# Attention on one core: the two rows that subtract each query's maximum, for two key tiles and both heads, as four 32-row products in a block of their own

## Chip, cores and metric

The kernel runs on one core of a Trainium2 chip. The metric is the device time of one launch in microseconds (us). Four stages follow each other in that launch: a state-space layer, a quantised linear layer, attention, and a mixture of experts. The change touches attention alone.

## Reference, cut to what matters

```python
x = (latents - mu) * jax.lax.rsqrt(var + 1e-05) * ln_gamma + ln_beta
q = (x @ Wq).reshape(b, s, HEADS, DIM_HEAD).transpose(0, 2, 1, 3)
...
scores = jnp.einsum('bhqd,bhkd->bhqk', q * scale, k * scale)
weights = jax.nn.softmax(scores.astype(jnp.float32), axis=-1).astype(scores.dtype)
out = jnp.einsum('bhqk,bhkd->bhqd', weights, v)
out = out.transpose(0, 2, 1, 3).reshape(b, s, HEADS * DIM_HEAD)
return out @ Wo
```

Here b = 2, s = 2048, 16 heads of 64. The softmax takes each query's maximal score off before the exponential.

## The kernel before, in words

Attention runs once for each of the two batch entries. `attention_first` makes the keys, queries and values of the first pair of heads; `attention_pairs` then does everything else in one long block. Its work is cut into groups `g` (a pair of heads and 512 queries: 8 pairs x 4 pieces = 32 groups) and within a group into 16 units `kt` (128 keys each). One unit is a score tile of 128 keys x 2 heads x 512 queries in two PSUM banks. The banks alternate, so units u and u+1 hold banks 0 to 3.

The order on TensorE (PE) is written out by hand, two units a turn, in the loop at the end of its block:

- `maxes(u)`: 2 products of 64 rows (one for each head, in two halves of the array's rows) that are read by VectorE (DVE) for the maxima of the next group (`find_max`, L976; `read_max`, L983). They wait until DVE has read the step before (`max_read`); there is only one pair of banks for it.
- `scores(u + 2)`, `scores(u + 3)`: four terms each (L1202): main keys x main queries, main x rest, rest x main, and `row_ones` x `row_shift`. The last term adds minus the maximum: `row_shift` holds it in two rows (a rough part and a correction) in rows 0, 1 for head 0 and 64, 65 for head 1; all other rows are zero. Each term is a pair of products of 64 rows. The unit's last product raises `s_psum`.
- `maxes(u + 1)`.
- `values(u)`, `values(u + 1)`: products of the exponentials `p` with v (L1213), 128 rows by 64 columns, one for each head; the trace shows two passes of each, so 8 to a turn.
- at six of a group's eight turns (`BANK7_AT`, by kt) one use of bank 7: the denominators (kt 2, L1224), the output product (kt 8, L1229), the turned shift of the next group (kt 10, `turn_shift`, L1000), or a projection of later heads (kt 0, 12, 14, L1009 or L1011). It waits for `bank7_free`.

ScalarE (ACT) makes `p` of a unit from its two banks (L1299) and copies bank 7 out where needed (the shift at L1273). GpSimd (POOL) adds the `p` of a group's 16 units up (L1323, 15 adds a group, eight `p` buffers deep). DVE reads each maximum step, and at kt 10 runs `make_shift` (L990 to L992) ahead of that unit's `read_max`; it also does `rest_part` (L1019) behind the read of an odd unit, which frees bank 7, and the steps of the division (L1344, L1345, L1351).

The semaphore of a score unit is counted by ACT:

```python
for i, (left, right) in enumerate(terms):
    for h in range(2):
        last = nc.tensor.matmul(s_bank(u)[:, piece(h)], left[hi(h)], right[hi(h)],
                                start=(i == 0), stop=(i == len(terms) - 1))
last.then_inc(s_psum, 1)
```

Of the kernel before, what the change touches and what calls it, by code (L numbers as in the profile page):

```python
# [17 lines left out]
BF16 = mybir.dt.bfloat16  # L18
U32 = mybir.dt.uint32
ALU = mybir.AluOpType  # L20
ACT = mybir.ActivationFunctionType
X_AXIS = mybir.AxisListType.X

P = 128
BANK = 512
# [3 lines left out]
TPC = BANK // P  # L29
# [795 lines left out]
def phase2(nc, ins, x_in, x_out, experts, ident, ident_bf, ones, exponent, psum):  # L825


    with Phase(nc) as ph:
        xaT = ph.sbuf("xaT", [P, SEQ])
        attnT = ph.sbuf("attnT", [P, SEQ])  # L830
        stat = ph.sbuf("stat2", [P, 4, TILES])
        six = ph.sbuf("six2", [P, TILES, 6])
        two = ph.sbuf("two2", [P, TILES, 2])
        gamma = ph.sbuf("gamma", [P, 1])
        beta = ph.sbuf("beta", [P, 1])
        w_qkv = ph.sbuf("w_qkv", [P, 2, 3, P])
        w_o = ph.sbuf("w_o", [P, 2, D])

        v = ph.sbuf("v", [P, 2, TILES, P])

        k_main = ph.sbuf("k_main", [P, 2, SEQ], F32R)
        k_rest = ph.sbuf("k_rest", [P, 2, SEQ], F32R)
        q_main = ph.sbuf("q_main", [P, 2, SEQ], F32R)
        q_rest = ph.sbuf("q_rest", [P, 2, SEQ], F32R)

        row_shift = ph.sbuf("row_shift", [P, 2, BANK], F32R)
        row_ones = ph.sbuf("row_ones", [P, P], F32R)  # L850
        quarters = ph.sbuf("quarters", [P, 2, 2, PAIR_MAXES])

        o_raw = ph.sbuf("o_raw", [P, BANK])
        den_g = ph.sbuf("den_g", [P, 2, 2, BANK])
        rec = ph.sbuf("rec", [P, BANK])
        newt = ph.sbuf("newt", [P, BANK])
        common = {k: x for k, x in locals().items() if k not in ("nc", "x_in", "x_out", "ins", "ph", "experts")}

        with Phase(nc) as su:
            zero_one = su.sbuf("zero_one", [P, 2])  # L860
            loaded, filled, cleared, step = (su.sem(s) for s in ("loaded", "filled", "cleared", "step"))
            with nc.Block() as block:
                @block.sync
                def _(sp):
                    sp.dma_start(gamma[:], ins["ln_gamma"]).then_inc(loaded, 16)
                    sp.dma_start(beta[:], ins["ln_beta"]).then_inc(loaded, 16)
                    sp.wait_ge(loaded, 32)

                @block.gpsimd
                def _(pool):  # L870
                    nc.gpsimd.memset(experts["down_b"][:], 0.0).then_inc(cleared, 1)
                    pool.wait_ge(cleared, 1)

                @block.vector
                def _(dve):
                    st = Steps(dve, step)

                    st.link(nc.vector.memset(zero_one[:, 0:1], 0.0))
                    st.link(nc.vector.memset(zero_one[:, 1:2], 1.0))
                    for i in range(2):  # L880
                        nc.vector.tensor_copy(row_shift[:, i, :], zero_one[:, 0:1].to_broadcast([P, BANK])).then_inc(filled, 1)
                    nc.vector.tensor_copy(row_ones[:], zero_one[:, 0:1].to_broadcast([P, P])).then_inc(filled, 1)
                    dve.wait_ge(filled, 3)
                    for h in range(2):
                        nc.vector.tensor_copy(row_ones[64 * h:64 * h + 2, :],
                                              zero_one[64 * h:64 * h + 2, 1:2].to_broadcast([2, P])).then_inc(filled, 1)
                    dve.wait_ge(filled, 5)
            nc.all_engine_barrier(sems_to_clear=sem_range(su.sems))

        for b in range(BATCH):  # L890
            attention_input(nc, ins, x_in, b, common)
            attention_first(nc, b, common, experts if b == 0 else None)
            attention_pairs(nc, ins, b, common)
            attention_output(nc, x_in, x_out, b, common)
# [54 lines left out]
PAIR_MAXES = TPC * CHUNKS  # L949

AHEAD = 6
SHIFT_MADE_AT = PAIR_MAXES - AHEAD

BANK7_AT = {0: 0, 2: "den", 8: "out", 10: "shift", 12: 1, 14: 2}
# [8 lines left out]
def hi(h):  # L963

    return slice(64 * h, 64 * h + 64)


def piece(c):
    return slice(c * BANK, (c + 1) * BANK)
# [16 lines left out]
def make_shift(nc, st, quarters, maxima, shift):  # L986


    each = quarters.rearrange("p h (j k) -> p (h j) k", k=CHUNKS)
    st.mark(nc.vector.tensor_reduce(maxima, each, X_AXIS, ALU.max, negate=True))  # L990
    st.link(nc.vector.tensor_reduce(shift[:, :, 0], each, X_AXIS, ALU.max, negate=True))
    return nc.vector.tensor_tensor(shift[:, :, 1], maxima, shift[:, :, 0], ALU.subtract)  # L992


def turn_shift(nc, dst, shift, ident_bf):

    for h in range(2):
        at = 64 * h
        for j in range(TPC):
            last = nc.tensor.matmul(dst[at:at + 2, j * P:(j + 1) * P], shift[:, h * TPC + j, :], ident_bf[:],  # L1000
                                    start=True, stop=True)
    return last

# [17 lines left out]

def attention_first(nc, b, m, experts):

    xaT, w_qkv, w_o, v, k_main, k_rest, q_main, q_rest, row_shift, quarters, ident_bf, psum = (
        m[k] for k in "xaT w_qkv w_o v k_main k_rest q_main q_rest row_shift quarters ident_bf psum".split())
    with Phase(nc, f"_{b}") as su:
        maxima = su.sbuf("maxima0", [P, 2 * TPC])
        shift = su.sbuf("shift0", [P, 2 * TPC, 2], BF16)
        (step, proj_psum, rounded, raw_ready, rest_done_v, rest_done_g, v_read, max_psum, max_read, shift_ready,
         shift_psum, shift_read) = (su.sem(s) for s in (  # L1030
            "step proj_psum rounded raw_ready rest_done_v rest_done_g v_read max_psum max_read shift_ready "
# [7 lines left out]
        km, kr, qm, qr = (t[:, 0] for t in (k_main, k_rest, q_main, q_rest))  # L1039
        with nc.Block() as block:  # L1040
# [39 lines left out]
            def _(act):  # L1080
# [10 lines left out]
                act.wait_ge(shift_psum, 1)  # L1091
                for h in range(2):
                    at = 64 * h
                    nc.scalar.copy(row_shift[at:at + 2, 0, :], psum[at:at + 2, 0:BANK]).then_inc(shift_read, 1)
                act.wait_ge(rounded, 2 * CHUNKS)
                act.wait_ge(v_read, CHUNKS)
                act.wait_ge(shift_read, 2)
# [18 lines left out]
def attention_pairs(nc, ins, b, m):  # L1116


    xaT, attnT, w_qkv, w_o, v, k_main, k_rest, q_main, q_rest, ones, ident_bf, psum = (
        m[k] for k in "xaT attnT w_qkv w_o v k_main k_rest q_main q_rest ones ident_bf psum".split())  # L1120
    row_shift, row_ones, quarters = (m[k] for k in "row_shift row_ones quarters".split())
    o_raw, den_g, rec = (m[k] for k in "o_raw den_g rec".split())
    GC = PAIRS * CHUNKS
    units = [(g, kt) for g in range(GC) for kt in range(KT)]
# [18 lines left out]
    with Phase(nc, f"_{b}") as su:  # L1143
        p = su.sbuf("p", [P, LIVE, 2, BANK])
        maxima = su.sbuf("maxima", [P, 2 * TPC])
        shift = su.sbuf("shift", [P, 2 * TPC, 2], BF16)
        (weights, out_weight, step, max_psum, max_read, shift_ready, shift_read, s_psum, p_ready, pv_done, added_g,
         o_copied, rec_rough, rec_step, rec_ready, o_ready, rounded, bank7_full, bank7_free) = (
            su.sem(s) for s in (
# [12 lines left out]
        with nc.Block() as block:  # L1162
# [16 lines left out]
            def _(pe):  # L1179
# [10 lines left out]
                def scores(u):  # L1190
                    g, kt = units[u]
                    km, kr, qm, qr = buffers(g, k_main, k_rest, q_main, q_rest)
                    if kt == 0 and g:
                        pe.wait_ge(shift_read, 2 * g)
                    if u >= 2:
                        pe.wait_ge(p_ready, u - 1)
                    keys, cols = slice(kt * P, (kt + 1) * P), piece(g % CHUNKS)
                    terms = [(km[:, keys], qm[:, cols]), (km[:, keys], qr[:, cols]), (kr[:, keys], qm[:, cols]),
                             (row_ones[:], row_shift[:, g % 2, :])]
                    for i, (left, right) in enumerate(terms):  # L1200
                        for h in range(2):
                            last = nc.tensor.matmul(s_bank(u)[:, piece(h)], left[hi(h)], right[hi(h)],  # L1202
                                                    start=(i == 0), stop=(i == len(terms) - 1))
                    last.then_inc(s_psum, 1)

                def values(u):
                    g, kt = units[u]
# [31 lines left out]

                scores(0)  # L1240
                scores(1)
                for u in range(0, len(units), 2):
                    maxes(u)
                    if u + 2 < len(units):
                        scores(u + 2)
                        scores(u + 3)
                    maxes(u + 1)
                    values(u)
                    values(u + 1)
                    if u in at_unit:  # L1250
                        use_bank7(at_unit[u])

            @block.scalar
            def _(act):
                nc.scalar.preload_act_table_set(EXP_LN)

                def read_bank7(k):
# [12 lines left out]
                    elif what == "shift":  # L1270
                        for h in range(2):
                            at = 64 * h
                            nc.scalar.copy(row_shift[at:at + 2, (g + 1) % 2, :], bank7[at:at + 2, :]).then_inc(shift_read, 1)  # L1273
                        act.wait_ge(shift_read, 2 * (g + 1))
                        nc.scalar.nop().then_inc(bank7_free, 1)
                    else:
# [541 lines left out]
```

## Time and profile before

| | us |
|---|---|
| median of 3 runs | 3752.65 (3745.63 to 3760.2) |
| the profiled execution, its own time | 3751.12 |
| its span, first to last instruction | 3749.0 |
| mean granted TensorE clock, share of full | 0.951 |

The span is one execution by the hardware profiler. PE is the matmul row, PEld the weight loads, which overlap it. A matmul's end is modelled, so its start is what to read: the distance of two starts is what a product takes. "Idle before" is time the engine stood, with what released it.

### The profile page before, as it was taken

To read this page: it belongs to the slowest core of one execution; us is meant where nothing else is said; L and a number is where in the kernel's file an instruction comes from. 1 tells how busy PE (TensorE), PEld (TensorE's weight loads), DVE (VectorE), ACT (ScalarE), POOL (GpSimd) and SP (SyncE) were. 2 spreads that over 40 slices of the span, in tenths; PEclk is the share of its full clock that TensorE was granted. 3 is DMA by queue.
4 is the path that set the end of the run, shared out by engine and by line. 5 is a ranking of instruction groups with operands and counts; after the bars stand their busy time and mean duration, and the time that the engine had idled before them with its cause. 6 is when DMAs were issued, how large, how long until landed. Compare 5 with 4: busy or idle time off the path is not lost. (4 is left out here: it accounts for less than half of the span.)

```text
span 3749.0 us, 48401 instructions
## 1 busy us (share of the span) xinstructions
PE 3371.6 (90%) x19041; PEld 1777.9 (47%) x19041; DVE 2386.7 (64%) x2724; ACT 1686.7 (45%) x2081; POOL 2762.5 (74%) x1154
## 2 busy tenths in 40 slices
PE   5774688289999999999999499999999999998898
PEld 2222233245554545555455245455554545554798
DVE  5998699766666666665664556656666666662554
ACT  4331433145454454454445244454445454454454
POOL 1883188158888888888889288888888888898233
PEclk9897798689999999999999799999999999998899
DMA  1330233010000000000000100000000000000000
GB/s 25 135 118 28 59 120 104 28 28 1 4 1 4 4 1 4 1 4 1 2 1 1 40 3 1 4 4 1 4 1 4 1 4 2 1 1 12 26 18 15
DMA packets 61535, 76.14 MB, mean 20 GB/s; under 512 B 7289, under 2 KB 48962, under 8 KB 61250
## 3 DMA queue, kind: packets, MB, share of 16 engines
q1 hardware_dynamic: 59362, 72.71, 6.1%
q8 instruction: 146, 2.39, 0.3%
q14 instruction: 75, 0.61, 0.1%
q10 hardware_dynamic: 1952, 0.43, 0.1%
HBM read 66.30 MB, written 6.82 MB: 20 GB/s over the span
## 5 line engine op out<-in xcount | busy, mean ns | idle before, releaser
L1323 POOL TENSOR_TENSOR den_g<-den_g,p 128x1024 f32<-128x1024 f32 x896 | 2128.6, 2376 | 288.5 <-ACT p L1299 183.0
L983 DVE TENSOR_REDUCE quarters<-psum 128x2 f32<-128x1024 f32 x1024 | 1250.6, 1224 | 939.3 <-PE psum L976 929.3
L1299 ACT ACTIVATE p<-psum 128x1024 f32<-128x1024 f32 x1024 | 994.5, 1023 | 725.4 <-PE psum L1202 717.3
L1213 PE MATMUL psum<-p,v 128*64 128x512 f32 x4096 | 991.6, 605 | 0.0
L976 PE MATMUL psum<-k_main,q_main 64*128 64x512 f32 x2048 | 462.4, 446 | 13.7 <-DVE quarters L983 11.2
L1213 PEld LDWEIGHTS psum<-p,v 128*64 128x64 f32 x4096 | 248.4, 136 | 470.0 <-issue 316.1
L1202 PE MATMUL psum<-q_main,k_main 64*128 64x512 f32 x2048 | 408.1, 394 | 4.5 <-PEq L1113 4.5
L1202 PE MATMUL psum<-q_rest,k_main 64*128 64x512 f32 x2048 | 405.1, 391 | 0.0
L1202 PE MATMUL psum<-q_main,k_rest 64*128 64x512 f32 x2048 | 404.8, 390 | 0.0
L1202 PE MATMUL psum<-row_shift,row_ones 64*128 64x512 f32 x2048 | 404.5, 390 | 0.0
L976 PEld LDWEIGHTS psum<-k_main,q_main 64*128 64x128 f32 x2048 | 193.7, 184 | 361.3 <-issue 198.6
L726 POOL TENSOR_TENSOR seen<-state,c_sb 128x2048 f32<-128x2048 f32 x64 | 285.2, 4457 | 68.6 <-DVE state L673 60.2
L611 PE MATMUL psum<-seen,ident 128*128 128x512 f32 x512 | 264.7, 654 | 26.9 <-POOL seen L726 26.8
L1202 PEld LDWEIGHTS psum<-q_main,k_main 64*128 64x128 f32 x2048 | 194.9, 186 | 42.3 <-issue 11.3
L1202 PEld LDWEIGHTS psum<-q_main,k_rest 64*128 64x128 f32 x2048 | 194.4, 185 | 43.1
L1202 PEld LDWEIGHTS psum<-q_rest,k_main 64*128 64x128 f32 x2048 | 194.4, 185 | 42.6
L1202 PEld LDWEIGHTS psum<-row_shift,row_ones 64*128 64x128 f32 x2048 | 194.2, 185 | 42.8
L1323 POOL TENSOR_TENSOR den_g<-p 128x1024 f32<-128x1024 f32 x64 | 151.0, 2360 | 55.4 <-ACT p L1299 54.2
L713 POOL TENSOR_TENSOR xnT<-dx,work 128x1024 f32<-128x1024 f32 x32 | 75.2, 2349 | 153.7 <-DMA work<-bc_rows 153.7
L611 PEld LDWEIGHTS psum<-seen,ident 128*128 128x128 f32 x512 | 96.2, 201 | 153.0 <-issue 103.5
L1009 PE MATMUL psum<-xaT,w_qkv 128*128 128x512 f32 x256 | 147.9, 667 | 6.9 <-PEq L942 4.0
L1775 POOL TENSOR_TENSOR mixed<-mixed,part 128x512 f32<-128x512 f32 x56 | 74.1, 1323 | 104.3 <-DVE part L1740 104.3
(253 smaller groups left out, 3298.2 us busy)
## 6 DMA issues: line engine op xcount, KB each, us to landing
c_sb<-bc_rows SPq DMA_DIRECT2D x64, 512.0 KB, 3.6
work<-bc_rows SPq DMA_DIRECT2D x32, 512.0 KB, 4.8
resid<-in_resid SPq DMA_DIRECT2D x8, 256.0 KB, 3.8
x_mid<-resid SPq DMA_DIRECT2D x8, 256.0 KB, 2.6
xa<-x_mid SPq DMA_DIRECT2D x8, 256.0 KB, 3.6
x_tok<-x_mid SPq DMA_DIRECT2D x8, 256.0 KB, 3.8
x_mid<-x_tok SPq DMA_DIRECT2D x8, 256.0 KB, 2.7
x<-x_mid SPq DMA_DIRECT2D x8, 256.0 KB, 2.8
```

The costliest lines, as they stand in the source:

```text
L611: last = nc.tensor.matmul(y_sum[:, h, k * BANK:(k + 1) * BANK], ident[:], seen[:, i % SLOTS, h, k * BANK:(k + 1) * BANK], start=False, sto ...
L713: nc.gpsimd.tensor_tensor(fed[:, k % SLOTS, :], dx[:, 1, s * SCAN:(s + 1) * SCAN], b_sb[:, k % SLOTS, :], ALU.mult).then_inc(fed_by_pool, 1)
L726: nc.gpsimd.tensor_tensor(seen[:, i % SLOTS, 0:halves], state[:, i % SLOTS, 0:halves], c_sb[:, i % C_SLOTS, :].unsqueeze(1).to_broadcast([ ...
L976: last = nc.tensor.matmul(max_banks[:, piece(h)], q[hi(h), c * BANK + j * P:c * BANK + (j + 1) * P], k[hi(h), piece(quarter)], start=True, ...
L983: return nc.vector.reduce_max(quarters[:, :, n], max_banks.rearrange("p (h k) -> p h k", h=2), X_AXIS)
L1009: return nc.tensor.matmul(dst, w[:, 1 - i // CHUNKS, :], xaT[:, piece(c)], start=True, stop=True)
L1202: last = nc.tensor.matmul(s_bank(u)[:, piece(h)], left[hi(h)], right[hi(h)], start=(i == 0), stop=(i == len(terms) - 1))
L1213: last = nc.tensor.matmul(o_bank[hi(h), :], vv[:, kt, hi(h)], p[:, u % LIVE, h, :], start=(kt == 0), stop=(kt == KT - 1))
L1299: nc.scalar.activation(flat(p[:, u % LIVE]), s_bank(u), ACT.Exp, scale=float(DH) ** -0.5).then_inc(p_ready, 1)
L1323: nc.gpsimd.tensor_tensor(sums, first, src, ALU.add).then_inc(added_g, 1)
L1775: nc.gpsimd.tensor_tensor(mixed[:, u % 2], x[:, u % 2] if e == 0 else mixed[:, u % 2], part[:, e % 2], ALU.add).then_inc(summed, 1)
```

## The change

Three things, all in attention:

- The fourth term leaves `scores`. `subtract_maxima(u)` does it for units u and u+1 and both heads as four products of 32 rows each, in the four quarters of the array's rows: quarter 2h + v takes head h of unit u + v. It stands once a turn, behind `maxes(u + 1)` and ahead of `values(u)`. One product of it raises `s_psum` by 2, so ACT hears of both units at once. The wait for the next group's shift moves there too.
- The two rows of each head are needed in two quarters now. `make_shift` writes columns 0, 1 and 32, 33 of a `shift` tile that is 34 wide and zero between: one reduction and one subtraction more. `turn_shift` turns 34 columns instead of 2, and ACT copies 34 rows instead of 2.
- `shift` is one tile of the whole stage, zeroed once by POOL, and `row_ones` gets its ones in four places instead of two, once.

```diff
-        shift = su.sbuf("shift", [P, 2 * TPC, 2], BF16)
+        shift = ph.sbuf("shift", [P, 2 * TPC, SHIFT_ROWS], BF16)
...
+                nc.gpsimd.memset(shift[:], 0.0).then_inc(cleared, 1)
...
-                    for h in range(2):
-                        nc.vector.tensor_copy(row_ones[64 * h:64 * h + 2, :],
+                    for r in range(4):
+                        nc.vector.tensor_copy(row_ones[32 * r:32 * r + 2, :],
...
+SHIFT_ROWS = 34
...
     st.mark(nc.vector.tensor_reduce(maxima, each, X_AXIS, ALU.max, negate=True))
-    st.link(nc.vector.tensor_reduce(shift[:, :, 0], each, X_AXIS, ALU.max, negate=True))
-    return nc.vector.tensor_tensor(shift[:, :, 1], maxima, shift[:, :, 0], ALU.subtract)
+    for at in (0, 32):
+        st.mark(nc.vector.tensor_reduce(shift[:, :, at], each, X_AXIS, ALU.max, negate=True))
+    st.wait()
+    st.mark(nc.vector.tensor_tensor(shift[:, :, 1], maxima, shift[:, :, 0], ALU.subtract))
+    return nc.vector.tensor_tensor(shift[:, :, 33], maxima, shift[:, :, 32], ALU.subtract)
...
-            last = nc.tensor.matmul(dst[at:at + 2, j * P:(j + 1) * P], shift[:, h * TPC + j, :], ident_bf[:],
+            last = nc.tensor.matmul(dst[at:at + SHIFT_ROWS, j * P:(j + 1) * P], shift[:, h * TPC + j, :], ident_bf[:],
...
-                    if kt == 0 and g:
-                        pe.wait_ge(shift_read, 2 * g)
...
-                             (row_ones[:], row_shift[:, g % 2, :])]
...
-                    last.then_inc(s_psum, 1)
+                def subtract_maxima(u):
+                    g, kt = units[u]
+                    if kt == 0 and g:
+                        pe.wait_ge(shift_read, 2 * g)
+                    for v in range(2):
+                        for h in range(2):
+                            rows = slice(64 * h + 32 * v, 64 * h + 32 * v + 32)
+                            last = nc.tensor.matmul(s_bank(u + v)[:, piece(h)], row_ones[rows, :], row_shift[rows, g % 2, :],
+                                                    start=False, stop=True)
+                    last.then_inc(s_psum, 2)
...
                 scores(1)
+                subtract_maxima(0)
                 for u in range(0, len(units), 2):
...
                     maxes(u + 1)
+                    if u + 2 < len(units):
+                        subtract_maxima(u + 2)
                     values(u)
...
-                            nc.scalar.copy(row_shift[at:at + 2, (g + 1) % 2, :], bank7[at:at + 2, :]).then_inc(shift_read, 1)
+                            nc.scalar.copy(row_shift[at:at + SHIFT_ROWS, (g + 1) % 2, :], bank7[at:at + SHIFT_ROWS, :]).then_inc(shift_read, 1)
```

## Rows read from the trace of the kernel before

**Rows 1.** Each engine's busy time, share of the span, instructions.

```profile
PE 3371.6 (90%) x19041; PEld 1777.9 (47%) x19041; DVE 2386.7 (64%) x2724; ACT 1686.7 (45%) x2081; POOL 2762.5 (74%) x1154
```

**Rows 2.** Busy time in a stretch of attention: PE, PEld, DVE, ACT, POOL, clock, DMA.

```profile
1000.00:1500.00 500.00, 498.72 (x3069) 253.35 (x3070) 312.69 (x308) 248.81 (x295) 436.99 (x185) 1.00 0.01 3
```

**Rows 3.** The costliest groups: count, busy us, mean ns, idle before.

```profile
L1323 POOL TENSOR_TENSOR den_g<-den_g,p 128x1024 f32<-128x1024 f32 x896 | 2128.6, 2376 | 288.5 <-ACT p L1299 183.0
L1202 PE MATMUL psum<-row_shift,row_ones 64*128 64x512 f32 x2048 | 404.5, 390 | 0.0
```

**Rows 4.** Timeline, one turn without bank 7 (kt 4): start us, us, engine.

```profile
1005.69 0.50 PE L976 MATMUL psum<-k_main,q_main 64*128 64x512 f32 x2
...
1006.03 0.40 PE L1202 MATMUL psum<-q_main,k_main 64*128 64x512 f32 x2
...
1006.24 1.23 DVE L983 TENSOR_REDUCE quarters<-psum 128x2 f32<-128x1024 f32 x1 [1.61 <-PE psum L976]
...
1007.16 1.94 ACT L1299 ACTIVATE p<-psum 128x1024 f32<-128x1024 f32 x2
...
1007.64 0.39 PE L1202 MATMUL psum<-row_shift,row_ones 64*128 64x512 f32 x2
1007.64 0.19 PEld L976 LDWEIGHTS psum<-k_main,q_main 64*128 64x128 f32 x2
1007.87 0.39 PE L976 MATMUL psum<-k_main,q_main 64*128 64x512 f32 x2
1008.18 0.20 PEld L1213 LDWEIGHTS psum<-p,v 128*64 128x64 f32 x4 [0.35 <-ACT p L1299]
...
1009.09 0.14 PEld L1213 LDWEIGHTS psum<-p,v 128*64 128x64 f32 x2 [0.29 <-issue]
...
1010.05 0.50 PE L976 MATMUL psum<-k_main,q_main 64*128 64x512 f32 x2
```

**Rows 5.** Timeline, the last two value products of that turn.

```profile
1009.52 0.60 PE L1213 MATMUL psum<-p,v 128*64 128x512 f32 x2
```

**Rows 6.** Timeline, the turn before it (kt 2), which ends with bank 7.

```profile
1002.70 0.20 PEld L1213 LDWEIGHTS psum<-p,v 128*64 128x64 f32 x4 [0.35 <-ACT p L1299]
...
1003.95 0.68 DVE L1019 TENSOR_TENSOR k_rest<-psum,k_main 128x512 fp32r<-128x512 f32 x1
1004.68 0.20 PEld L1224 LDWEIGHTS psum<-den_g,ones 128*64 128x64 f32 x4 [0.93 <-DVE k_rest L1019]
```

**Rows 7.** Waits, whole span: us in total, times, longest.

```profile
PEld psum L1009 <- DVE q_rest L1019: 26.1, 28, 0.9
...
PEld psum L1224 <- DVE k_rest L1019: 24.3, 26, 0.9
```

**Rows 8.** The instructions of line 992: shortest, median, longest ns.

```profile
L992 DVE TENSOR_TENSOR shift<-maxima,shift x64: 170/2100/2144, 780.9 to 3401.4; 128x8 bf16<-128x8 f32 x64
```

**Rows 9.** Timeline, `make_shift` and the turn of kt 10.

```profile
1018.35 4.90 POOL L1323 TENSOR_TENSOR den_g<-den_g,p 128x1024 f32<-128x1024 f32 x2
1018.36 0.19 DVE L990 TENSOR_REDUCE maxima<-quarters 128x8 f32<-128x32 f32 x1
1018.46 0.18 DVE L991 TENSOR_REDUCE shift<-quarters 128x8 bf16<-128x32 f32 x1
1018.67 2.07 DVE L992 TENSOR_TENSOR shift<-maxima,shift 128x8 bf16<-128x8 f32 x1
...
1019.90 0.50 PE L976 MATMUL psum<-k_main,q_main 64*128 64x512 f32 x2
...
1020.66 1.21 DVE L983 TENSOR_REDUCE quarters<-psum 128x2 f32<-128x1024 f32 x1
```

**Rows 10.** Timeline, later in that turn.

```profile
1021.92 0.19 PEld L976 LDWEIGHTS psum<-k_main,q_main 64*128 64x128 f32 x2
1022.08 0.39 PE L976 MATMUL psum<-k_main,q_main 64*128 64x512 f32 x2
```

**Rows 11.** Timeline, POOL's next add.

```profile
1020.86 2.40 POOL L1323 TENSOR_TENSOR den_g<-den_g,p 128x1024 f32<-128x1024 f32 x1
```

More of the change, by code:

```diff
@@ L871, in _ @@
                     nc.gpsimd.memset(experts["down_b"][:], 0.0).then_inc(cleared, 1)
-                    pool.wait_ge(cleared, 1)
+                    nc.gpsimd.memset(shift[:], 0.0).then_inc(cleared, 1)
+                    pool.wait_ge(cleared, 2)
                 @block.vector
@@ L883, in _ @@
                     dve.wait_ge(filled, 3)
-                    for h in range(2):
-                        nc.vector.tensor_copy(row_ones[64 * h:64 * h + 2, :],
-                                              zero_one[64 * h:64 * h + 2, 1:2].to_broadcast([2, P])).then_inc(filled, 1)
-                    dve.wait_ge(filled, 5)
+                    for r in range(4):
+                        nc.vector.tensor_copy(row_ones[32 * r:32 * r + 2, :],
+                                              zero_one[32 * r:32 * r + 2, 1:2].to_broadcast([2, P])).then_inc(filled, 1)
+                    dve.wait_ge(filled, 7)
             nc.all_engine_barrier(sems_to_clear=sem_range(su.sems))
@@ L1022, in attention_first @@
 def attention_first(nc, b, m, experts):
-    xaT, w_qkv, w_o, v, k_main, k_rest, q_main, q_rest, row_shift, quarters, ident_bf, psum = (
-        m[k] for k in "xaT w_qkv w_o v k_main k_rest q_main q_rest row_shift quarters ident_bf psum".split())
+    xaT, w_qkv, w_o, v, k_main, k_rest, q_main, q_rest, row_shift, quarters, shift, ident_bf, psum = (
+        m[k] for k in "xaT w_qkv w_o v k_main k_rest q_main q_rest row_shift quarters shift ident_bf psum".split())
     with Phase(nc, f"_{b}") as su:
         maxima = su.sbuf("maxima0", [P, 2 * TPC])
-        shift = su.sbuf("shift0", [P, 2 * TPC, 2], BF16)
         (step, proj_psum, rounded, raw_ready, rest_done_v, rest_done_g, v_read, max_psum, max_read, shift_ready,
@@ L1093, in _ @@
                     at = 64 * h
-                    nc.scalar.copy(row_shift[at:at + 2, 0, :], psum[at:at + 2, 0:BANK]).then_inc(shift_read, 1)
+                    nc.scalar.copy(row_shift[at:at + SHIFT_ROWS, 0, :], psum[at:at + SHIFT_ROWS, 0:BANK]).then_inc(shift_read, 1)
                 act.wait_ge(rounded, 2 * CHUNKS)
@@ L1120, in attention_pairs @@
         m[k] for k in "xaT attnT w_qkv w_o v k_main k_rest q_main q_rest ones ident_bf psum".split())
-    row_shift, row_ones, quarters = (m[k] for k in "row_shift row_ones quarters".split())
+    row_shift, row_ones, quarters, shift = (m[k] for k in "row_shift row_ones quarters shift".split())
     o_raw, den_g, rec = (m[k] for k in "o_raw den_g rec".split())
@@ L1197, in scores @@
                     keys, cols = slice(kt * P, (kt + 1) * P), piece(g % CHUNKS)
-                    terms = [(km[:, keys], qm[:, cols]), (km[:, keys], qr[:, cols]), (kr[:, keys], qm[:, cols]),
-                             (row_ones[:], row_shift[:, g % 2, :])]
+                    terms = [(km[:, keys], qm[:, cols]), (km[:, keys], qr[:, cols]), (kr[:, keys], qm[:, cols])]
                     for i, (left, right) in enumerate(terms):
                         for h in range(2):
-                            last = nc.tensor.matmul(s_bank(u)[:, piece(h)], left[hi(h)], right[hi(h)],
-                                                    start=(i == 0), stop=(i == len(terms) - 1))
-                    last.then_inc(s_psum, 1)
+                            nc.tensor.matmul(s_bank(u)[:, piece(h)], left[hi(h)], right[hi(h)], start=(i == 0), stop=False)
+                def subtract_maxima(u):
[8 more added lines that the diff above has]
+                    last.then_inc(s_psum, 2)
                 def values(u):
```

## The prediction

> **What bounds the kernel.** I read the page's busy shares first: PE 90%, POOL 74%, DVE 64%, ACT 45% [rows 1]. These are averages over four stages, so I then read the busy time of stretches inside attention. There PE is busy for 498.7 of 500 us at the full granted clock (2.4 GHz) and POOL for 437 [rows 2]. Attention's line 992 runs from 780.9 to 3401.4 [rows 8], so some 2600 us of the span go at PE's pace. A microsecond taken from PE's list in a turn is a microsecond of the end, until something else ends last. The next candidate is POOL: an add takes 2.38 us, and the next starts 2.51 behind it [rows 3, 9, 11], so 185 instructions fill 464 of the 500 us. Attention can lose 7% before POOL is the bound. The list of costly groups gives the term that is moved: 2048 products of `row_shift`, none with idle time before it [rows 3].
>
> Then the timeline of one plain turn, for starts alone [rows 4, 5]. From its first `maxes` to the next turn's are 4.36 us. Pairs of 64-row products stand 0.23 us apart (1006.03 to 1007.64 is seven of them). Value pairs stand 0.43 apart (1009.09 to 1009.52). And the places where the array's division changes cost more than a pair: values to `maxes` 1009.52 to 1010.05 is 0.53 for a pair of 0.43, and the first `maxes` pair to the first score pair 0.34 for a pair of 0.23. In the other direction, `maxes` to values is 1007.87 to 1008.18, 0.31 for 0.23.
>
> **The change part by part.**
>
> *Shift products.* A turn has two pairs of them, 0.46 us. In their place stands one block of four products in four quarters. Two halves run side by side now (both starts within one row of the timeline); if four quarters do so too, the block takes 0.23. Gain 0.23 a turn, 512 turns: **-118 us**.
>
> *The block's own entry.* Before, the turn had two changes of division: 128 rows to 64, and 64 rows to 128 x 64. Now it has three: 128 to 64, 64 to 32 rows, 32 rows to 128 x 64. The trace has no change from 64 to 32 rows. Nearest is the one into a row division, 128 to 64: 0.10 before the first product and 0.11 on it, because the weights of 128 columns are loaded in the open; 0.21 together [rows 4, 5]. The block loads 128 columns as well. I take 0.21: **+108 us**. Lower bound 0, if quarters count as the same division as halves. Middle bound the other direction's 0.08 and 0.05 (0.13), with 64 columns to load: +67. Upper bound 0.32, if the four weight loads go two by two and the open load doubles: +164.
>
> The Trainium skill ("TensorEngine Tiling (Array Packing)", § Key Properties) says that a change of tiling mode drains TensorE, while another tile of one mode does not. By that rule the three changes each drain, which is the 0.21 taken and not the lower bound of 0; the page has no price for a drain, and this trace's changes agree that each costs something.
>
> *Stalls on bank 7.* After an odd `read_max`, DVE runs `rest_part` (0.68 us), and only then is bank 7 free. At 1004.63 it ends, and PE's load for L1224 starts at 1004.68 [rows 6]. Without it the values, begun at 1002.70, would let it start 1.77 later (as 1008.18 to 1009.52 plus 0.43), at 1004.47. So PE stands 0.21. There are 26 such waits in one row for L1224 and 14 in a second row behind `q_rest`; for L1009 28, and another 28 behind `k_rest` [rows 7]. Those of L1009 need a new division anyway, which takes 0.10 of the 0.21, so they cost about 0.11: 40 x 0.21 + 56 x 0.11 = 14.6, and a few of L1011, 16 in all. In the changed turn the block stands between `maxes(u + 1)` and the values and makes PE 0.44 later there (0.23 + 0.21), while DVE's chain hangs on `maxes(u + 1)` alone. The stalls go: **-16 us**. If the entry costs nothing, PE is 0.23 later and they go just as well.
>
> *The read between the two `maxes`.* `maxes(u + 1)` may load its weights when DVE has read the step before. DVE starts 0.55 behind `maxes(u)`, reads 1.23 and ends at 1007.47; the load stands at 1007.64, of which 0.05 is the semaphore's way (as 1004.63 to 1004.68) [rows 4, 6]. So 0.12 is spare. With the pair gone the load wants to start 0.23 earlier and is 0.11 late. But it is issued 0.23 ahead of its product, and needs some 0.11 of these (the open load above), so it can be 0.12 late for nothing. At kt 10 this is seen: the load at 1021.92, only 0.16 ahead of its product at 1022.08, with no pair pushed out [rows 10]. I cost it at nothing; the cover is nearly used up.
>
> *Exponentials.* The first unit's signal now comes with the second's. Before, ACT starts at 1007.16, 1.47 into the turn. Now the block starts 1.72 + 0.31 = 2.03 into it, and ACT 0.54 behind (as DVE behind the first `maxes`), at 2.6. Two exponentials of 1.94 in all end at 4.5 [rows 4]. The next turn's second score unit needs the second one's end, and its load would stand 0.8 into that turn, at 5.1. Spare 0.6. POOL gets its `p` 1.1 later, with eight buffers and 7% to spare. ACT's bank 7 work comes after the turn's end, behind 4.5. Cost nothing.
>
> *The shift's own path.* `make_shift` has one reduction more (0.10, L990 to L991) and one subtraction more. A subtraction takes 170 ns at best and 2100 in the median [rows 8]. The reason stands in the timeline: L992 starts at 1018.67 and ends at 1020.74, as POOL's add begun at 1018.35 ends (2.38 later, 1020.73). It waits for the add, then, though no semaphore joins the two [rows 9]. So what the second one costs depends on who is next. DVE's next instruction starts at 1020.66, POOL's next add at 1020.86 [rows 9, 11]. A second subtraction of 0.17 from 1020.66 on would end at 1020.83, just before. I take it as fitting the gap: 0.1 us on DVE, ahead of a read that in this kernel starts 0.2 late without harm. If it doesn't fit, it waits for a whole add (a rival, below).
>
> *The rest.* `turn_shift` turns 34 columns instead of 2, eight times a group: between -0.10 a group (a division nearer to that of the values) and +0.2 (longer loads in the open), -6 to +12 us over all; I take 0. ACT's copies have 512 elements a row as before. The wait for the next group's shift stands in the same turn of kt 14 as before, but 1.7 us later in it, so the copy has more time than before; the values would be queued behind it. Three small instructions of preparation, once: under 1 us.
>
> **Sum:** -118 + 108 - 16 = -26 us, from the profiled execution's 3751.1 to 3725. The median of the runs lies 1.5 above that execution: 3726.5.
>
> **The rivals.**
>
> *R1, the second subtraction waits for a whole add of POOL* (the other side). It would then end 2.51 behind the first. The first ends 0.84 into the turn of kt 10 now (1020.74 less 1019.90 [rows 9]). The adds move 1.1 later against the turn with the exponentials, and an add's end then falls at 0.84 + 1.1 - 2.51, 0.57 ahead of the turn; the first takes that one, the second the next, 1.94 into the turn. The read starts at 1.86 instead of 0.55 and ends at 3.1, the load follows at 3.15, the product 0.11 later at 3.26 instead of 1.72: 1.5 late, once a group. About 55 of 64 groups have POOL busy there (median 2100 ns [rows 8]): +83, **3809 us**. For it: the gap is only 0.14 to 0.2 us. Against: DVE asks first. The Trainium skill ("SBUF — State Buffer", § Who interferes with whom) states a lock on a shared port pair that the first to start holds for its whole instruction; the 2.1 against 0.17 us agrees, and asking first would spare the second subtraction. It decides if the second subtraction takes over 1 us.
>
> *R2, entering quarters is free.* Then only the gain stands: -118 - 16, **3618 us**. Against: every change of division that the trace has costs something.
>
> *R3, four quarters don't run side by side at full pace.* If two by two, the block takes 0.46: +118, 3844 us; half of that, **3785 us**. For it: the trace shows no more than two row parts, and four would write four PSUM banks at a time. Against: two parts lose nothing.
>
> The Trainium skill ("TensorE: Matmul & The Clock Gate", § Measured speedup vs the span model) gives 3.07 times for four row tiles, not 4. An estimate from that: the block would take 0.30 and not 0.23, the sum some +10, 3763 us.
>
> *R4, the maximum's read becomes a wait.* If a late load isn't hidden, each turn loses 0.11 at `maxes(u + 1)`: +55, **3781 us**. It decides when DVE's read ends later than some 1.8 into the turn.
>
> **Numbers.** Forecast (entry at about 0.21, the rest hidden) 50%, with its own range 3700 to 3748: the entry's price is uncertain by 0.04 a turn or 20 us. R1 15%, R2 10%, R3 14%, R4 8%, others 3%. The 8 in 10 range leaves out R2 and the far end of R3: 3690 to 3815. A measurement of this kernel can tell some 0.5% from no change, 19 us, so under 3734 is faster. Of the forecast's 50 some 32 lie there, with R2 and others 44%. Slower (over 3771): R1, most of R3, two thirds of R4 and little else, 30%. The same: 26%.
>
> **What would show it.** Right: a plain turn of about 4.34 us; the block's first start 0.31 behind `maxes`, the values some 0.43 behind that; no start on L1224 waiting for `rest_part`; the second subtraction at 0.1 to 0.2 us. Wrong: values 0.65 or more behind the block (R3), a second subtraction of 2 us with DVE's read of kt 10 late (R1), the load of `maxes(u + 1)` right behind DVE's end with its product pushed out (R4), a block start 0.23 behind `maxes` (R2), or a POOL that never idles in a group.

## The result and the profile after

The changed kernel takes 3820.88 us (median of 4 runs, 3817.73 to 3825.63) against 3752.06 for the kernel before on the same chip: 1.0179 times as long, 95% interval 1.0166 to 1.0193. It is 69 us slower, where 26 us faster was forecast.

First the busy time of the stretch of attention that [rows 2] show of before (PE, PEld, DVE, ACT, POOL, clock), and the group of the moved products:

```profile
1000.00:1500.00 500.00, 500.00 (x2996) 230.65 (x2992) 293.15 (x324) 240.81 (x287) 425.65 (x181) 1.00 0.01 3
```

```profile
L1217 PE MATMUL psum<-row_shift,row_ones 32*128 32x512 f32 x2048 | 259.7, 497 | 0.0
```

PE is "busy" for all 500 us, more than the 498.7 of before, and yet does fewer products in them (2996 for 3069; POOL 181 instructions for 185). The granted clock is the same, 1.00 of full. A matmul's end is modelled, and one that waits for its weights is drawn longer (497 ns here, 390 in [rows 3]), so such a stall can't be seen in the busy share or in "idle before". It is seen in the starts. Timeline of the changed kernel, one turn, here with a bank 7 use at its end:

```profile
1007.20 0.50 PE L981 MATMUL psum<-k_main,q_main 64*128 64x512 f32 x2
...
1007.54 0.39 PE L1206 MATMUL psum<-q_main,k_main 64*128 64x512 f32 x2
...
1007.74 1.23 DVE L988 TENSOR_REDUCE quarters<-psum 128x2 f32<-128x1024 f32 x1 [1.97 <-PE psum L981]
...
1008.69 0.40 PE L1206 MATMUL psum<-q_main,k_rest 64*128 64x512 f32 x2
1009.02 0.19 PEld L981 LDWEIGHTS psum<-k_main,q_main 64*128 64x128 f32 x2 [0.37 <-DVE quarters L988]
1009.02 0.51 PE L981 MATMUL psum<-k_main,q_main 64*128 64x512 f32 x2
1009.46 0.19 PEld L1217 LDWEIGHTS psum<-row_shift,row_ones 32*128 32x128 f32 x4 [0.25 <-issue]
1009.46 0.51 PE L1217 MATMUL psum<-row_shift,row_ones 32*128 32x512 f32 x4
...
1009.90 0.20 PEld L1228 LDWEIGHTS psum<-p,v 128*64 128x64 f32 x4 [0.25 <-issue]
...
1010.01 1.94 ACT L1317 ACTIVATE p<-psum 128x1024 f32<-128x1024 f32 x2 [2.12 <-PE psum L1217]
```

Read against [rows 4]. The first `maxes` to the first score pair: 0.34, as before. The last score pair to the second `maxes`: 1008.69 to 1009.02, 0.33 where pairs stand 0.23 apart. The weights of `maxes` are loaded at 1009.02, not a pair earlier, and this is 0.05 behind the end of DVE's read (1007.74 + 1.23 = 1008.97). Second `maxes` to the block: 0.44, where 0.31 was expected. Block to values: 0.44, as expected.

The waits of the whole span, as [rows 7] show them of before, and the two subtractions of the shift (ns, shortest, median, longest), for [rows 8]:

```profile
PEld psum L981 <- DVE quarters L988: 227.0, 548, 0.8
...
PEld psum L1239 <- DVE k_rest L1028: 12.9, 26, 0.5
```

```profile
L999 DVE TENSOR_TENSOR shift<-maxima,shift x64: 194/756/1260, 786.9 to 3475.1; 128x8 bf16<-128x8 f32 x64
```

```profile
L1000 DVE TENSOR_TENSOR shift<-maxima,shift x64: 178/180/186, 787.0 to 3476.2; 128x8 bf16<-128x8 f32 x64
```

DVE's read now releases the load of `maxes` 548 times, once a turn and some, for 227.0 us of idle load; before it was 172 times and 120.0 us. The loads of the denominators (L1224 before) stand idle 12.9 us in 26 waits instead of 24.3, 0.44 less each, which is what the block ahead of the values takes on PE. The second subtraction never waits.

### The profile page after: what moved, and what is told of

It is laid out like the page before. It is cut to its first block and busy times, and to the rows that moved or that the text cites. A ratio compares the mean times of both kernels' runs of the same rounds, so it can differ in the third digit from the quotient of the medians.

```text
span 3821.3 us, 48470 instructions
## 1 busy us (share of the span) xinstructions
PE 3450.7 (90%) x19041; PEld 1689.3 (44%) x19041; DVE 2340.1 (61%) x2854; ACT 1680.6 (44%) x2081; POOL 2763.2 (72%) x1155
## 5 line engine op out<-in xcount | busy, mean ns | idle before, releaser
L981 PE MATMUL psum<-k_main,q_main 64*128 64x512 f32 x2048 | 512.9, 497 | 14.3 <-DVE quarters L988 11.6
L1217 PE MATMUL psum<-row_shift,row_ones 32*128 32x512 f32 x2048 | 259.7, 497 | 0.0
L1217 PEld LDWEIGHTS psum<-row_shift,row_ones 32*128 32x128 f32 x2048 | 98.0, 181 | 128.3 <-issue 128.3
```

The lines of the kernel that those rows point to most:

```text
L981: last = nc.tensor.matmul(max_banks[:, piece(h)], q[hi(h), c * BANK + j * P:c * BANK + (j + 1) * P], k[hi(h), piece(quarter)], start=True, ...
L1217: last = nc.tensor.matmul(s_bank(u + v)[:, piece(h)], row_ones[rows, :], row_shift[rows, g % 2, :], start=False, stop=True)
```

## The experiments

Theory A, formed on these rows: the change took *two* pairs of products out of the stretch between a turn's two maximum steps (the fourth term of both score units), so the second step now waits for DVE. Rival B: the block of quarters, or its late signal to ACT, is what costs. Each experiment below is held against the kernel before, run beside it on the same chip.

**Shorter read, in the changed kernel.** DVE reads 256 of 512 scores a head; the maxima of the other keys are left out.

```diff
-    return nc.vector.reduce_max(quarters[:, :, n], max_banks.rearrange("p (h k) -> p h k", h=2), X_AXIS)
+    return nc.vector.reduce_max(quarters[:, :, n], max_banks.rearrange("p (h k) -> p h k", h=2)[:, :, 0:256], X_AXIS)
```

> The changed kernel, but DVE's maximum read takes 256 of each head's 512 scores (the maxima of the other half of the keys are left out), so it is some 0.55 us shorter and can't hold the second maximum step. Theory A (two score pairs, not one, left the stretch between the two maximum steps, so the second one now waits for DVE's read, 0.10 us a turn, and its weights are loaded in the open, 0.11 more): some 490 turns give back 0.21 us each, 3821 to about 3718. Rival B (the cost lies in the block of four quarters itself or in its late signal to ACT): the read plays no part, 3800 to 3825.

**The control: the same edit in the kernel before.**

> The control: the kernel before with the same shortened read. No turn waits for the read there, so both theories expect only what the earlier freeing of bank 7 gives: 3752 to about 3736. If it drops by much more, the read held the kernel before too and the first experiment can't be put down to the new wait.

Measured: 3710.4 us in the changed kernel, 0.9892 of before (0.9875 to 0.9908), 110 us under the changed one. The control: 3720.4, 0.9921 (0.9905 to 0.9938). The timeline of a plain turn (one without bank 7) of the first:

```profile
1006.69 0.50 PE L981 MATMUL psum<-k_main,q_main 64*128 64x512 f32 x2
1007.23 0.69 DVE L988 TENSOR_REDUCE quarters<-psum 128x2 f32<-128x512 f32 x1 [0.71 <-PE psum L981]
...
1008.19 0.19 PEld L981 LDWEIGHTS psum<-k_main,q_main 64*128 64x128 f32 x2
1008.41 0.39 PE L981 MATMUL psum<-k_main,q_main 64*128 64x512 f32 x2
1008.73 0.19 PEld L1217 LDWEIGHTS psum<-row_shift,row_ones 32*128 32x128 f32 x4 [0.35 <-issue]
...
1009.17 0.20 PEld L1228 LDWEIGHTS psum<-p,v 128*64 128x64 f32 x4 [0.25 <-issue]
...
1011.03 0.51 PE L981 MATMUL psum<-k_main,q_main 64*128 64x512 f32 x2
```

The load stands 0.22 ahead of its product again, `maxes` to block is 0.32, and the turn 4.34 us: what the prediction had said of the changed kernel. The block and its late signal are still there, so B is out as the cause of the loss. The control fell by 29 where 16 was expected. Most of the rest lies ahead of the turns: from the first maximum step to the first value product that kernel takes 26.8 us, the kernel before 34.0, in each of the two batch entries. The changed kernel gains there too: 35.2 and 35.1 us fall to 30.2 and 27.9, 12 in all. So not all of its 110 us is the wait. The wait's own share is read in the turns: the 486 that each trace has from one first `maxes` to the next take 2518.6 us in the changed kernel and 2418.0 with the short read, 0.21 less each (2453.1 before, 2431.7 in the control). Lines 976 and 1213 of the control; the two times behind the durations are the first and the last start:

```profile
L976 PE MATMUL psum<-k_main,q_main x2048: 383/492/790, 766.2 to 3367.9; 64*128 64x512 f32 x187
```

```profile
L1213 PEld LDWEIGHTS psum<-p,v x4096: 132/137/137, 793.0 to 3413.3; 128*64 128x64 f32 x196
```

With the short read in both, the changed kernel is 10.0 us ahead. About 5 of these lie in the turns of kt 10, where the wider shift is turned (60 of them, 4.60 us on average against 4.69). A plain turn takes 4.35 us on average against 4.38. So the block itself wins a few hundredths of a us a turn at most, as the prediction's two large terms have it (118 - 108 = 10 us).

**The move alone.** The kernel before, its fourth term behind the second `maxes`, as two pairs of 64 rows.

```diff
-                    terms = [..., (row_ones[:], row_shift[:, g % 2, :])]
...
+                def subtract_maxima(u):
...
+                    for v in range(2):
+                        for h in range(2):
+                            last = nc.tensor.matmul(s_bank(u + v)[:, piece(h)], row_ones[hi(h)], row_shift[hi(h), g % 2, :],
+                                                    start=False, stop=True)
+                    last.then_inc(s_psum, 2)
```

> The kernel before with the shift's products moved behind the second maximum step but left as two pairs of 64 rows (no quarters, no new division of the array, one signal for both units, 2 columns of shift). Theory A: the stretch between the maximum steps is as short as in the changed kernel, the wait of 0.10 and the open load of 0.11 are both paid, the stalls on bank 7 go: 3752 + 105 - 16 = about 3840. Rival B (quarters are what costs): near 3740.

Measured: 3843.2, 1.0247 (1.023 to 1.0264), as expected. The move alone costs 94 us, with no quarter in it. From its timeline:

```profile
1008.82 0.40 PE L1199 MATMUL psum<-q_main,k_rest 64*128 64x512 f32 x2
1009.14 0.19 PEld L976 LDWEIGHTS psum<-k_main,q_main 64*128 64x128 f32 x2 [0.36 <-DVE quarters L983]
1009.14 0.49 PE L976 MATMUL psum<-k_main,q_main 64*128 64x512 f32 x2
...
1009.48 0.63 PE L1207 MATMUL psum<-row_shift,row_ones 64*128 64x512 f32 x4
```

0.32 to the second `maxes` and 0.34 from it to the next pair, for 0.23 each: 0.09 of waiting and 0.11 of load in the open.

**Quarters ahead of the second maximum step.**

```diff
-                    maxes(u + 1)
                     if u + 2 < len(units):
                         subtract_maxima(u + 2)
+                    maxes(u + 1)
```

> The changed kernel with the block of quarters ahead of the second maximum step instead of behind it. The distance between the two maximum steps is long enough again, so no wait for the read, but the array is divided anew four times a turn instead of three (32 rows back to 64). Theory A with a division at 0.20 us: a plain turn of 4.55 us against 4.56 in the changed kernel and some stalls on bank 7 back, 3820 to 3835. If going from 32 to 64 rows were free, about 3735.

Measured: 3845.7, 1.0252 (1.0235 to 1.0269), slower than expected. Its timeline:

```profile
905.46 0.39 PE L1206 MATMUL psum<-q_main,k_rest 64*128 64x512 f32 x2
905.78 0.19 PEld L1217 LDWEIGHTS psum<-row_shift,row_ones 32*128 32x128 f32 x4 [0.36 <-issue]
...
906.22 0.50 PE L981 MATMUL psum<-k_main,q_main 64*128 64x512 f32 x2
...
906.65 0.20 PEld L1228 LDWEIGHTS psum<-p,v 128*64 128x64 f32 x4 [0.25 <-issue]
...
908.43 0.19 DVE L999 TENSOR_TENSOR shift<-maxima,shift 128x8 bf16<-128x8 f32 x1
...
908.52 2.37 DVE L1000 TENSOR_TENSOR shift<-maxima,shift 128x8 bf16<-128x8 f32 x1
909.57 0.19 PEld L981 LDWEIGHTS psum<-k_main,q_main 64*128 64x128 f32 x2 [0.76 <-issue]
...
910.79 1.21 DVE L988 TENSOR_REDUCE quarters<-psum 128x2 f32<-128x1024 f32 x1
...
912.06 0.49 PE L981 MATMUL psum<-k_main,q_main 64*128 64x512 f32 x2 [0.17 <-DVE quarters L988]
```

The wait for the read is gone in a plain turn, but each of the block's two borders costs: 0.32 into it, and 0.44 and 0.43 behind it for products of 0.23. Of 0.44, 0.11 is the open load and 0.10 the change of division. So quarters ask for some 0.20 a time at either place. The plain turn comes out at 4.55 us, as expected; what was not expected lies in the other turns. The rival R1 of the prediction turns up, in the second part of the rows: POOL's add starts at 908.43, as the first subtraction does. The first is through in 0.19, the second meets the add and takes 2.37, and the read of kt 10 and the second `maxes` (2.49 behind the first) are late. So it goes in 36 of the 64 groups. The stalls on bank 7 are back too, 0.93 us of idle load each as before. POOL's row in the same timeline, and the waits of the span:

```profile
908.43 2.40 POOL L1341 TENSOR_TENSOR den_g<-den_g,p 128x1024 f32<-128x1024 f32 x1
```

```profile
PEld psum L1239 <- DVE k_rest L1028: 24.2, 26, 0.9
```

**That kernel with one subtraction over two columns**, to try R1.

```diff
-    st.mark(nc.vector.tensor_tensor(shift[:, :, 1], maxima, shift[:, :, 0], ALU.subtract))
-    return nc.vector.tensor_tensor(shift[:, :, 33], maxima, shift[:, :, 32], ALU.subtract)
+    return nc.vector.tensor_tensor(shift[:, :, 1:34:32], maxima.unsqueeze(2).to_broadcast([P, 2 * TPC, 2]),
+                                   shift[:, :, 0:33:32], ALU.subtract)
```

> The kernel with the block of quarters ahead of the second maximum step, and both subtractions of the shift as one instruction over two columns. In the run with two, the first was mostly free (0.19 us) and the second waited for POOL's add (median 2.37), which held the read of kt 10 and made that turn 5.03 us instead of 4.78. If it is the second instruction's wait (the rival R1 of the prediction), one instruction is free here and the turn of kt 10 falls to about 4.78: 0.25 x 60, 3846 to about 3831. If the adds just stand in another phase and the one instruction waits as well, 3846.

Measured: 3844.5, 1.0244 (1.0229 to 1.026). Inconclusive as to the time, where 3831 was expected: in 37 of the 64 groups the one instruction was free, in the other 27 it met the add itself. The turn of kt 10 does show R1's price: 4.78 us in the median, with the instruction free, against 5.03 with two subtractions, and 4.86 against 4.99 on average, 8 us in 60 turns. Which way it goes is a matter of hundredths of a us: where the add had started 0.01 to 0.03 us ahead of the subtraction this took 2.4 us, where it started just behind it 0.20.

```profile
L999 DVE TENSOR_TENSOR shift<-maxima,shift x64: 202/205/2422, 783.3 to 3494.8; 128x16 bf16<-128x16 f32 x64
```

**A wait between the two subtractions, in the changed kernel.**

```diff
-    st.mark(nc.vector.tensor_tensor(shift[:, :, 1], maxima, shift[:, :, 0], ALU.subtract))
+    st.link(nc.vector.tensor_tensor(shift[:, :, 1], maxima, shift[:, :, 0], ALU.subtract))
```

> The changed kernel with a semaphore wait between the two subtractions of the shift. In the changed kernel the second takes 0.18 us each time. If what saved it is that it asks for its input ahead of POOL's next add, the wait's some 0.1 us lets the add in: the second subtraction then takes up to 2.4 us in groups where the first waited for an add, and DVE's read behind it is late. If the two never compete, 0.18 again.

Measured in a single run: 3819.0 us. The second subtraction:

```profile
L1000 DVE TENSOR_TENSOR shift<-maxima,shift x64: 194/196/197, 784.5 to 3471.4; 128x8 bf16<-128x8 f32 x64
```

Still free, so the wait did not let the add in. The semaphore moved the second subtraction 0.14 us back, and it still starts 0.05 us ahead of POOL's next add and ends while this is under way. A subtraction behind one that has waited for an add gets through in POOL's gap, with room for a semaphore. What waits is the instruction that comes while an add is under way.

**The block doubled, with zero weights first.**

```diff
+                    for ones_or_none in (row_none, row_ones):
...
-                            last = nc.tensor.matmul(s_bank(u + v)[:, piece(h)], row_ones[rows, :], row_shift[rows, g % 2, :],
-                                                    start=False, stop=True)
+                                last = nc.tensor.matmul(s_bank(u + v)[:, piece(h)], ones_or_none[rows, :],
+                                                        row_shift[rows, g % 2, :], start=False, stop=(ones_or_none is row_ones))
```

> The changed kernel with the block of four quarters doubled: four more products with zero weights ahead of the four, in the same division. It prices the block without its entry. If four quarters run side by side at full pace: 0.23 us a turn, 512 turns, 3821 + 117 = about 3938. If two by two: +236, about 4057.

Measured: 3934.8, 1.0481 (1.0465 to 1.0497): 114 us over the changed kernel, 0.22 a turn, which is what one pair of halves takes. Four quarters run side by side at full pace, and R3 is out. Its timeline has the first block's open load (0.34 to the second) and the change to the values (0.33):

```profile
1001.76 0.50 PE L1220 MATMUL psum<-row_shift,row_none 32*128 32x512 f32 x4
...
1002.10 0.40 PE L1220 MATMUL psum<-row_shift,row_ones 32*128 32x512 f32 x4
1002.43 0.20 PEld L1231 LDWEIGHTS psum<-p,v 128*64 128x64 f32 x4 [0.37 <-issue]
```

**The kernel before with the second maximum step one pair earlier.**

```diff
                     for i, (left, right) in enumerate(terms):
+                        if i == len(terms) - 1 and ahead_of_shift is not None:
+                            maxes(ahead_of_shift)
                         for h in range(2):
...
-                        scores(u + 3)
-                    maxes(u + 1)
+                        scores(u + 3, u + 1)
+                    else:
+                        maxes(u + 1)
```

> The kernel before with the second maximum step one pair earlier, ahead of the last shift pair of the second score unit. It tests the cover: its load then waits for DVE's read 0.11 us, of which the 0.12 by which a load may be late should hide all; and DVE's chain behind it frees bank 7 0.23 us earlier, so its stalls go. Cover as reckoned: 3752 - 16 = about 3736. Cover too short: up to 0.1 us a turn lost, up to 3790.

**The same with 34 columns of shift**, 32 of them zero (ACT copies two rows as before, one subtraction).

> The kernel before with the second maximum step one pair earlier (as in the run before) and the shift turned with 34 columns instead of 2, 32 of them zero, so that its products stand in the division of the values ahead of them (the changed kernel shows 0.42 instead of 0.52 us there). 0.10 us a group more off: about 3730, if the early step gives its 16.

Measured: 3749.2, 0.9991 (0.9982 to 1.0), and 3742.3, 0.9968 (0.9956 to 0.998). The early step gave 3 us, not 16. The lead of the load covers the wait, as reckoned: in a plain turn the load starts 0.13 ahead of its product instead of 0.22, no product is late, and the turn stays at 4.38 us on average. The stall on bank 7 is gone as well, which gives some 15 us. But the turn of kt 10 is not free: 4.89 us on average instead of 4.70, 12 us in 60 turns. Timeline of the second of these kernels there:

```profile
980.47 2.35 DVE L996 TENSOR_TENSOR shift<-maxima,shift 128x8 bf16<-128x8 f32 x1
981.93 0.19 PEld L980 LDWEIGHTS psum<-k_main,q_main 64*128 64x128 f32 x2 [0.76 <-issue]
...
982.71 1.21 DVE L987 TENSOR_REDUCE quarters<-psum 128x2 f32<-128x1024 f32 x1
...
983.98 0.19 PEld L980 LDWEIGHTS psum<-k_main,q_main 64*128 64x128 f32 x2 [0.37 <-DVE quarters L987]
```

The subtraction starts just after an add of POOL has started, and takes as long as that does; the read begins 0.78 into the turn instead of the 0.55 of a plain turn, and the load waits for it, now that the spare time is spent.

**And with the subtraction on POOL**, in its queue behind the add of kt 10.

```diff
                     nc.gpsimd.tensor_tensor(sums, first, src, ALU.add).then_inc(added_g, 1)
                     n += 1
+                    if kt == SHIFT_MADE_AT and g + 1 < GC:
+                        pool.wait_ge(reduced, 2 * (g + 1))
+                        nc.gpsimd.tensor_tensor(shift[:, :, 1], maxima[:], shift[:, :, 0], ALU.subtract).then_inc(shift_ready, 1)
```

> The kernel with the early maximum step and the wide turned shift, and the shift's subtraction on POOL, in its queue behind the add of kt 10, instead of on DVE. In the run without this the subtraction waited 2.34 us on DVE and the turn of kt 10 took 4.82 us instead of some 4.60. If that wait is what ate the 16 us of the freed bank 7, 0.22 x 60 = 13 us come back: 3742 to about 3729, 0.6% below the kernel before. If not, 3742.

Measured: 3737.6, 0.9954 (0.994 to 0.9967), the fastest of the kernels that compute everything. Its timeline at kt 10:

```profile
983.33 0.50 PE L980 MATMUL psum<-k_main,q_main 64*128 64x512 f32 x2
983.87 1.23 DVE L987 TENSOR_REDUCE quarters<-psum 128x2 f32<-128x1024 f32 x1 [2.04 <-PE psum L980]
984.10 0.24 POOL L1332 TENSOR_TENSOR shift<-maxima,shift 128x8 bf16<-128x8 f32 x1
...
985.14 0.19 PEld L980 LDWEIGHTS psum<-k_main,q_main 64*128 64x128 f32 x2
985.28 0.39 PE L980 MATMUL psum<-k_main,q_main 64*128 64x512 f32 x2
985.71 1.23 DVE L987 TENSOR_REDUCE quarters<-psum 128x2 f32<-128x1024 f32 x1
```

The read starts 0.54 into the turn, the load is back 0.14 ahead of its product. The turns of kt 10 fall from 4.79 to 4.61 us on average, 11 us in 60 of them, near the 13 expected. Of these the whole kernel shows about 5 (0.9954 against 0.9968, each held against its own runs of the kernel before, and with intervals that overlap); where the rest went stays open.

## Why the prediction was wrong

The step that failed is "The read between the two `maxes`". It says: "With the pair gone the load wants to start 0.23 earlier and is 0.11 late", and costs that at nothing. Between the two `maxes` of a turn lie both score units, and each lost its shift pair. The load wants to start 0.46 earlier, 1.49 into the turn, and DVE's read lets it go at 1.82. It is 0.33 late, of which 0.12 is hidden by the lead of a load over its product; 0.21 is left, twice what R4 asked for. The paragraph on exponentials had the right figure, the second `maxes` at 1.72 into the turn, which is 0.46 and not 0.23 earlier than before; the two weren't set against each other.

Term by term:

- Shift products, -118: held. The doubled block cost 114.
- Entry into quarters, +108: held, though 0.21 was carried over from another change of division. With the wait gone, `maxes` to block is 0.32 and block to values 0.44 in the plain turn, and the turn 4.34 us.
- Stalls on bank 7, -16: held. In the move alone, and in the changed kernel, they are gone; in the kernel with quarters ahead of the step they are back. The 16 may be somewhat low: the turns of the control gained 21 us.
- Read between the steps, 0: was 0.21 us a turn, in some 490 turns (those with a second maximum step), +103. The short read took 101 us out of the 486 turns of the trace.
- Exponentials, 0: held. ACT starts 2.81 into the turn and ends its two at 4.75, later than the 4.5 reckoned by the same 0.21.
- Second subtraction, nothing: held here (0.18 us each time). R1's mechanism is real and hangs on where POOL's add stands: in the kernel with quarters ahead it cost the turn of kt 10 0.25 us where it struck.
- `turn_shift`, 0 within -6 to +12: its first product stands 0.42 behind the last value pair instead of 0.52, so at 62 groups it gave 6 us, the near bound.

With the mended terms: -118 + 108 - 16 - 6 + 103 = +71. Measured +69. That the two meet within 2 us is partly luck, since the terms are good to a few us each.

R4 was the right rival, at half its price and with a chance of only 8%. One of its signs was right: the load of `maxes(u + 1)` right behind DVE's end, with its product pushed out. The other was not ("when DVE's read ends later than some 1.8 into the turn"): that end did not move, it stands 1.78 into the turn before and 1.77 after, and yet each turn waits. The need for it moved. With two pairs gone, the load is late for nothing up to 1.49 + 0.12 = 1.61 into the turn, so the read would have to end by 1.56.

The Trainium skill ("TensorEngine Tiling (Array Packing)", § Key Properties) says that a change of tiling mode drains TensorE. The runs agree that such a change costs, from 64 to 32 rows and from 32 to 64: about 0.10 us each, besides 0.11 for a load that isn't made ahead across it. The estimate from the 3.07 times of the Trainium skill ("TensorE: Matmul & The Clock Gate", § Measured speedup vs the span model) would have made the block 0.30 us; the doubled block shows 0.22.

## What to carry to other kernels

When work is taken out of a hand-written order, count what leaves each stretch between two uses of a single buffer, not what leaves the loop: a reader on another engine doesn't get faster, and the time saved in that stretch comes back as a wait for it, with the next weight load in the open on top. Packing products into more, smaller row tiles saves one product's time and pays a change of division at the border (here 0.23 against 0.20), so it should be worth doing only where several such products stand together. The doubled block shows the second one at 0.22 with no border of its own; no run here shows a kernel that gains by it and computes everything.

## What the runs showed of the hardware

- A weight load may come late by some of its lead of 0.23 us over its product: 0.09 late cost nothing (the kernel with the early step, 4.38 us a turn as before), and 0.12 is what the sums give. When it was 0.33 late, the product started 0.10 later, and its own load in the open added 0.11: 0.21 us a turn.
- A DVE instruction of 0.2 us with two SBUF inputs takes up to 2.4 when it comes during a POOL add, while one that follows it takes 0.18 to 0.20, even behind a semaphore. The same two instructions can change places: first free, second caught (2.37 in the median). A start 0.01 us ahead of the add or behind it decides. The Trainium skill ("SBUF — State Buffer", § Who interferes with whom) has this as a lock that the first to start keeps; both pictures agree.
- PE's busy time rose from 498.7 to 500 us of 500 in attention while the products done in it fell from 3069 to 2996.
